# A decoder layer whose exponentials two engines share: a VectorE unit in every chunk, and the accumulators turned straight from their banks

## The chip, the cores and the metric

One core of one Trainium2 chip. The metric is the device time of one execution in microseconds (us). A time of the kernel is the median of its runs.

## The reference, cut to what matters

One decoder layer on x (1024 rows of 128) with a context of 6404 rows of 128. Three parts follow one another: a small self-attention with layer norm, a cross-attention with 16 heads of depth 8 over the context, and a quantised feed-forward part. The change is in the cross-attention, which takes most of the time:

```
qh = split_heads(q @ Wq + bq); kh = split_heads(k @ Wk + bk); vh = split_heads(v @ Wv + bv)
logits = einsum('bhsd,bhtd->bhst', qh, kh) / sqrt(8)      # 16 heads x 1024 x 6404
attn = softmax(logits, axis=-1)
out = einsum('bhst,bhtd->bhsd', attn, vh)                 # then @ Wo + bo
```

The kernel makes exp(logits) without a row maximum (a bound on the scores is computed first; a general path exists that these inputs don't take), multiplies it with the values and a column of ones, and divides by the sum that this column gives.

## The kernel before, in words

**Tiling.** The cross-attention is a stream of 8 phases: a phase is one half of the queries (512 columns) and a group of 4 heads (16 heads, so 4 groups; `PHASES` = 8). The context is 51 tiles of 128 rows (the last one short), 3 tiles to a chunk, so 17 chunks a phase (`NC`). A *unit* of scores is one tile for one head: 128 x 512 in one PSUM bank. Three units are a *block* (`BU`), 4 blocks a chunk (`BPC`), and the last chunk has 3 (`LAST_BPC`), since in its last tile the few rows of all four heads are packed into one unit. So a phase is 67 blocks (`BPP`), and the stream 536.

**Banks.** Blocks take turns in banks 0 to 2 and 3 to 5. Banks 6 and 7 (`ACC`) are the accumulators of the values.

**Who does what.** For every block TensorE multiplies the scores (`scores`, 12 matmuls, L1544) into its three banks; ScalarE takes the exponential of the three banks in one instruction (`exponentials`, L801, 128 x 1536) and writes it to `probs`, a ring of 8 blocks; TensorE multiplies `probs` with the values of the previous chunk (`values`, L1574). In `chunk`, TensorE's order for block s is written out by hand: wait, scores of block s, then a share of the values of the chunk before. The scores of a block wait for ScalarE to have finished the block two before it (`probs_ready`).

**VectorE's units.** In one block of a chunk, the third (`E_BLOCK` = 2), the last bank isn't ScalarE's: ScalarE's instruction there covers 128 x 1024 (`shared`, L805), and VectorE makes the exponential of that bank with a polynomial in 12 instructions, six steps of two halves of 256 columns. `take(ph, c)` (L1134) reads the bank in the first four (L1142 `e_t`, L1148 `e_f`); then the bank is free. `power(ph, c)` (L1152) does the rest (L1159, L1164, L1170, L1175) and writes into `probs`. GpSimd makes the power of two from `e_t` (`powers`, L667). Each of the first ten instructions raises `e_step` by one; each of the last two raises `e_probs`. Before, chunk 1 and the last chunk of a phase have no such unit: `e_count(ph, c)` counts 15 units a phase, 120 in all.

**What TensorE waits for.** At s = 0 of every chunk but the first of a phase it waits until the take of the chunk before is done (`E_TAKEN` = 4 steps), and before the values that read a unit's result it waits for `e_probs`:

```
if s == 0 and c:
    wait(e_step, at(E_STEPS * (e_count(ph, c - 1) - 1) + E_TAKEN, E_STEPS))
wait(probs_ready, at(f + s + 1, BPC))
...
scores(m % KS, q, ph, c == NC - 1, s)
```

In chunk 1 (before) this wait on chunk 0's take is the last of its phase's start, and at the start of chunk 2 `e_count(ph, 1)` gives the same unit of chunk 0 again.

**The end of a phase.** The values of the last chunk are multiplied in chunk 0 of the next phase, one tile each in its blocks 0, 1 and 2. Then VectorE adds the two accumulator banks into `acc_sb` (`add_acc`, L1125, between the take and the power of chunk 0), and after the power of chunk 0 turns them, divides and turns back (`turn_acc`, L1180, and L1198); SP stores the rows. TensorE begins the new phase's values at (c = 1, s = 1) and before them waits for the two steps of `add_acc` (`acc_step`, ACC_STEPS * (ph - 1) + 2). GpSimd stages the values of each chunk (`stage`, L660) and makes the powers, in the order of chunks.

## Time and profile before

| | us |
|---|---|
| median of 3 runs (782.94 to 783.8) | 783.37 |
| the profiled execution's own time | 783.59 |
| its span, first to last instruction | 781.9 |
| ScalarE busy | 730.6 |
| TensorE busy | 702.9 |
| VectorE busy | 601.3 |
| GpSimd busy | 179.7 |

The span is a little shorter than the time, as it leaves out what lies before the first and after the last instruction. Busy time of TensorE is modelled from matmuls that overlap, so a share of 90% doesn't say how far it is from its own limit. L801 is line 801 of the kernel before.

### The profile page before, as it was taken

The numbers are of one execution on the slowest core, as the hardware profiler recorded it, in microseconds if no ns is written. First come the engines' busy times: TensorE is split into PE (matmuls) and PEld (weight loads), VectorE is DVE, ScalarE is ACT, GpSimd is POOL, SyncE is SP. The second block draws the span as 40 slices with busy tenths as digits, with TensorE's granted clock in tenths as the row PEclk, the third lists the DMA queues.
The fourth block names the chain that finished last, engine by engine and source line by source line (L and its number), as shares of the span: only waits on it lengthen the run. The fifth ranks groups of instructions, "written<-read, shape, count | busy, mean of one in ns | idle before, by whom it ended". The sixth has DMA issues, their size and how long they took to land.

```text
span 781.9 us, 36725 instructions
## 1 busy us (share of the span) xinstructions
PE 702.9 (90%) x15175; PEld 315.3 (40%) x15179; DVE 601.3 (77%) x1719; ACT 730.6 (93%) x651; POOL 179.7 (23%) x322
## 2 busy tenths in 40 slices
PE   9998999999999999899998999999998999899985
PEld 4564344334443444344433443344433443344342
DVE  4668688858885888678867888588867886788877
ACT  3467999999999999999999999999999999999964
POOL 4437122212221222112211222122212222122201
PEclk9999999999999999999999999999999999999998
DMA  5364111111111111111111111111111111111000
GB/s 140 118 179 161 36 47 36 37 43 43 37 37 41 48 39 34 39 47 42 36 40 43 44 35 37 45 46 36 37 40 46 42 35 40 39 37 36 14 2 27
DMA packets 37044, 38.37 MB, mean 49 GB/s; under 512 B 8968, under 2 KB 35402, under 8 KB 36948
## 3 DMA queue, kind: packets, MB, share of 16 engines
q1 hardware_dynamic: 35840, 36.52, 15.7%
q8 instruction: 65, 1.06, 0.6%
q10 hardware_dynamic: 1108, 0.53, 0.2%
q14 instruction: 31, 0.25, 0.1%
HBM read 30.14 MB, written 6.42 MB: 47 GB/s over the span
## 4 chain that ended last, share of the span: by engine, by line
ACT 57%; issue 26%; PE 10%; DVE 3%; ACTq 1%; DMA 1%; DVEq 0%; POOL 0%; POOLq 0%
ACT probs L801 57%; PE ps L1438 2%; PE ps L1391 1%; PE ps L1399 1%; PE ps L1429 1%; PE ps L1574 1%; DMA wq_sb<-in_L_xattn_Wq_dram 1%; PE ps L1382 1%; ACTq L814 1%; PE ps L1544 1%; PE ps L1364 1%; DVE gmax L1241 0%; ACTq L799 0%; DVE probs L1301 0%; DVE stats L906 0%
## 5 line engine op out<-in xcount | busy, mean ns | idle before, releaser
L801 ACT ACTIVATE probs<-ps 128x1536 f32<-128x1536 f32 (+1 forms) x536 | 669.4, 1392 | 2.0 <-PE ps L1544 1.9
L1574 PE MATMUL ps<-probs,v_op 64*9 64x512 f32 (+1 forms) x8256 | 522.9, 496 | 0.0
L1544 PE MATMUL ps<-q_op,k_op 59*32 59x512 bf16 x6432 | 332.8, 379 | 62.0 <-ACT probs L801 59.6
L1544 PEld LDWEIGHTS ps<-q_op,k_op 59*32 59x32 bf16 x6432 | 102.2, 89 | 347.0 <-issue 257.0
L1142 DVE TENSOR_SCALAR e_t<-ps 128x256 f32<-128x256 f32 x240 | 90.7, 420 | 140.9 <-PE ps L1544 140.9
L1574 PEld LDWEIGHTS ps<-probs,v_op 64*9 64x9 f32 x8256 | 171.6, 86 | 61.4 <-issue 4.3
L667 POOL TENSOR_SCALAR e_pow<-e_t 128x512 int32<-128x512 int16 x120 | 74.6, 622 | 356.3 <-DVE e_t L1142 356.3
L660 POOL COPY v_op<-v_all 128x108 f32<-128x108 f32 x136 | 64.7, 476 | 167.5 <-PE ps L1574 167.0
L1170 DVE SCALAR_TENSOR_TENSOR e_f<-e_f,e_pow 128x256 f32<-128x256 f32 x240 | 98.5, 449 | 0.0
L1164 DVE SCALAR_TENSOR_TENSOR e_f<-e_u,e_f 128x256 f32<-128x256 f32 x240 | 90.2, 416 | 0.0
L1159 DVE SCALAR_TENSOR_TENSOR e_u<-e_f 128x256 f32<-128x256 f32 x240 | 90.0, 416 | 0.2
L1175 DVE SCALAR_TENSOR_TENSOR probs<-e_u,e_f 128x256 f32<-128x256 f32 x240 | 89.6, 411 | 0.0
L1148 DVE SCALAR_TENSOR_TENSOR e_f<-ps,e_t 128x256 f32<-128x256 f32 x240 | 89.3, 414 | 0.0
L737 ACT ACTIVATE probs<-ps,neg_n 128x1024 f32<-128x1024 f32 x8 | 8.9, 1114 | 18.9 <-PE ps L1429 18.9
L961 DVE SCALAR_TENSOR_TENSOR probs<-ps,bias_cols,k_parts 128x384 f32<-128x384 f32 x17 | 10.5, 615 | 17.7 <-ACT k_parts L723 10.3
L1364 PE MATMUL ps<-zeros_bf 128*128 128x512 bf16 x48 | 15.6, 455 | 1.5 <-DVE zeros_bf L932 1.3
L621 POOL TENSOR_TENSOR k_parts<-probs,k_parts 128x384 bf16<-128x384 f32 x17 | 15.5, 914 | 1.4
L1391 PE MATMUL ps<-ctx_t,wk_turned 128*128 128x384 f32 x34 | 14.8, 518 | 0.7 <-DVE probs L961 0.7
L619 POOL CAST k_parts<-probs 128x384 bf16<-128x384 f32 x17 | 8.6, 505 | 29.4 <-DVE probs L961 29.2
L1438 PE MATMUL ps<-probs,x_nat 128*128 128x512 f32 x32 | 15.1, 593 | 0.0
L1399 PEld LDWEIGHTS ps<-wv_sb,ctx_t 128*128 128x128 f32 x102 | 13.6, 191 | 3.4 <-issue 0.5
L1399 PE MATMUL ps<-wv_sb,ctx_t 128*128 128x128 f32 x102 | 14.0, 275 | 0.0
(201 smaller groups left out, 265.4 us busy)
## 6 DMA issues: line engine op xcount, KB each, us to landing
k_op<-k_parts_dram SPq DMA_DIRECT2D x544, 36.0 KB
k_parts_dram<-k_parts SPq DMA_DIRECT2D x17, 288.0 KB, 2.9
k_op<-k_parts_dram SPq DMA_DIRECT2D x272, 12.0 KB
ctx_nat<-in_ctx_dram SPq DMA_DIRECT2D x16, 192.0 KB, 3.3
q_op<-q_parts_dram SPq DMA_DIRECT2D x32, 48.0 KB
q_parts_dram<-q_parts SPq DMA_DIRECT2D x2, 384.0 KB, 3.5
x_nat<-in_x_dram SPq DMA_DIRECT2D x1, 512.0 KB, 3.9
o_t<-att_rows SPq DMA_DIRECT2D x28, 16.0 KB
```

The costliest lines, as they stand in the source:

```text
L660: pool.tensor_copy(v_op[:, slot].rearrange("p j (h d) -> p j h d", h=G), v_all[:, bass.ds(tile, CT), head:head + G, :]).then_inc(v_staged, 1)
L667: pool.tensor_scalar(e_pow[:], e_low(e_t[:]), float(2 ** 23), float(EXP2_LEAD), ALU.mult, ALU.add).then_inc(e_pow_ready, 1)
L801: act.activation(probs[:, b % NP].rearrange("p u t -> p (u t)")[:, 0:columns], ps[:, bank:bank + BU, :].rearrange("p u t -> p (u t)")[:, 0 ...
L1142: dve.tensor_scalar(e_t[:, cols], score, E_MIN, ROUND + EXP2_OFF, ALU.max, ALU.add).then_inc(e_step, 1)
L1148: dve.scalar_tensor_tensor(out=e_f[:, cols], in0=score, scalar=E_MIN, in1=e_low(e_t[:, cols]), op0=ALU.max, op1=ALU.subtract).then_inc(e_s ...
L1159: dve.scalar_tensor_tensor(out=e_u[:, cols], in0=e_f[:, cols], scalar=a, in1=e_f[:, cols], op0=ALU.add, op1=ALU.mult).then_inc(e_step, 1)
L1164: dve.scalar_tensor_tensor(out=e_f[:, cols], in0=e_u[:, cols], scalar=d, in1=e_f[:, cols], op0=ALU.add, op1=ALU.mult).then_inc(e_step, 1)
L1170: dve.scalar_tensor_tensor(out=e_f[:, cols], in0=e_f[:, cols], scalar=e, in1=e_pow[:, cols].bitcast(F32), op0=ALU.add, op1=ALU.mult).then_ ...
L1175: dve.scalar_tensor_tensor(out=probs[:, block % NP, BU - 1, 512 - EW + cols.start:512 - EW + cols.stop], in0=e_u[:, cols], scalar=b, in1=e ...
L1399: last = pe.matmul(ps[:, v_bank(n), P * j:P * j + P], ctx_t[:, n % 3, P * j:P * j + P], wv_sb[:], start=True, stop=True)
L1544: return pe.matmul(ps[a:a + P // G, bank, :], k_op[W2 * r:W2 * r + KR, kslot, i, P * j + a:P * j + a + P // G], q_op[W2 * r:W2 * r + KR, q ...
L1574: last = pe.matmul(ps[32 * k:32 * k + DH + 1, ACC[h], a:b], v_op[W2 * h:W2 * h + W2, slot, j, (DH + 1) * k:(DH + 1) * (k + 1)], probs[W2 * ...
```

## The change

It does four things.

- `E_UNITS` goes from 15 to 17: VectorE makes a unit in every chunk. Only the last chunk of the last phase has none (`e_made`). In chunk 1 the unit is the last bank of the fourth block (`e_block(1)` = 3), in the others it stays in the third. ScalarE's instructions there shrink to 128 x 1024, and GpSimd makes a power of two for each new unit.
- TensorE gets a wait at (c = 0, s = 1) for the take of the last chunk of the phase before. Its wait at s = 0 of every other chunk stays as it is.
- The values of the packed tile (the last tile of the last chunk) are multiplied in block 3 of chunk 0 and no longer in block 2, behind a wait for the last chunk's unit.
- The accumulators are no longer copied and added, then turned: VectorE turns each from its bank (`turn_acc`, two transposes of 128 x 512, between the first and the second factor of chunk 0's unit), adds the kept columns and takes the reciprocal after chunk 2's unit (`divide_acc`), multiplies after chunk 3's (`normalise_acc`), and turns back after chunk 4's (`turn_rows`). `power` is split into `first_factor`, `second_factor` and `power`, with the same instructions. `ACC_STEPS` stays 5, and TensorE's wait for two steps now covers the two transposes.

```diff
--- before.py
+++ after.py
@@ -78,7 +78,7 @@
 EW = 512
 EH = EW // 2
 E_BLOCK = BPC - 2
-E_UNITS = NC - 2
+E_UNITS = NC
 EXP2_OFF = 2
 EXP2_LEAD = 0x3a8bec00 - EXP2_OFF * 2 ** 23
 EXP2 = [9.525652885437012, 28.199888229370117, 45.54460906982422, 132.23011779785156]
@@ -302,7 +302,15 @@
 
         def e_count(ph, c):
 
-            return ph * E_UNITS + max(c - 1, 0) + 1
+            return ph * E_UNITS + c + 1
+
+        def e_block(c):
+
+            return BPC - 1 if c == 1 else E_BLOCK
+
+        def e_made(ph, c):
+
+            return c < NC - 1 or ph < PHASES - 1
 
         def e_low(ap):
 
@@ -671,7 +679,7 @@
                 for c in range(NC):
                     m = ph * NC + c
                     stage(m % 2, m, c * CT, ph % NG * G)
-                    if c != 1 and c < NC - 1:
+                    if e_made(ph, c):
                         powers(ph, c)
 
 
@@ -802,20 +810,21 @@
                                ps[:, bank:bank + BU, :].rearrange("p u t -> p (u t)")[:, 0:columns],
                                ACT.Exp, scale=1.0 / LOG2E).then_inc(probs_ready, 1)
 
-            def shared(s):
-                return BU * 512 - EW if s == E_BLOCK else BU * 512
+            def shared(s, c=0):
+                return BU * 512 - EW if s == e_block(c) else BU * 512
 
             for ph in range(PHASES):
                 f = ph * BPP
                 for s in range(BPC):
                     exponentials(f + s, f + (s + 1 + AHEAD), shared(s))
                 for s in range(BPC, 2 * BPC):
-                    exponentials(f + s, f + (s + 1 + AHEAD))
-                with act.Fori(0, E_UNITS // 2) as r:
+                    exponentials(f + s, f + (s + 1 + AHEAD), shared(s - BPC, 1))
+                with act.Fori(0, (NC - 3) // 2) as r:
                     for s in range(2 * BPC, 4 * BPC):
                         exponentials(f + s, r * (2 * BPC) + (f + s + 1 + AHEAD), shared(s % BPC))
                 for s in range((NC - 1) * BPC, BPP):
-                    exponentials(f + s, f + (s + 1 + AHEAD))
+                    exponentials(f + s, f + (s + 1 + AHEAD),
+                                 shared(s % BPC) if e_made(ph, NC - 1) else BU * 512)
 
 
             act.preload_act_table(ACT.Sqrt)
@@ -1122,18 +1131,18 @@
             with dve.If(dve.value_load(flag[0:1, 0:1]) > 0):
                 general_shift_dve(dve)
 
-            def add_acc(ph):
+            def turn_acc(ph):
 
                 dve.wait_ge(values_done, V_AHEAD + VPC * NC * (ph + 1))
-                acc_chain.step(dve.tensor_copy(acc_sb[:], ps[:, ACC[0], :]))
-                acc_chain.step(dve.tensor_tensor(acc_sb[:], acc_sb[:], ps[:, ACC[1], :], ALU.add))
+                acc_chain.step(dve.transpose(acc_t[:].rearrange("p n d -> p (n d)"), ps[:, ACC[0], :]))
+                acc_chain.step(dve.transpose(acc_sb[:], ps[:, ACC[1], :]))
 
             acc_chain = Chain(dve, acc_step)
             halves = (slice(0, EH), slice(EH, EW))
 
             def take(ph, c):
 
-                block = ph * BPP + c * BPC + E_BLOCK
+                block = ph * BPP + c * BPC + e_block(c)
                 bank = BU * (block % 2) + BU - 1
                 done = E_STEPS * (e_count(ph, c) - 1)
                 dve.wait_ge(scores_done, block + 1 + AHEAD)
@@ -1149,21 +1158,29 @@
                                              in1=e_low(e_t[:, cols]), op0=ALU.max, op1=ALU.subtract
                                              ).then_inc(e_step, 1)
 
-            def power(ph, c):
-
-                block = ph * BPP + c * BPC + E_BLOCK
+            def first_factor(ph, c):
+
                 done = E_STEPS * (e_count(ph, c) - 1)
-                a, b, d, e = EXP2
                 for n, cols in enumerate(halves):
                     dve.wait_ge(e_step, done + 2 + n + 1)
-                    dve.scalar_tensor_tensor(out=e_u[:, cols], in0=e_f[:, cols], scalar=a,
+                    dve.scalar_tensor_tensor(out=e_u[:, cols], in0=e_f[:, cols], scalar=EXP2[0],
                                              in1=e_f[:, cols], op0=ALU.add, op1=ALU.mult
                                              ).then_inc(e_step, 1)
+
+            def second_factor(ph, c):
+
+                done = E_STEPS * (e_count(ph, c) - 1)
                 for n, cols in enumerate(halves):
                     dve.wait_ge(e_step, done + 4 + n + 1)
-                    dve.scalar_tensor_tensor(out=e_f[:, cols], in0=e_u[:, cols], scalar=d,
+                    dve.scalar_tensor_tensor(out=e_f[:, cols], in0=e_u[:, cols], scalar=EXP2[2],
                                              in1=e_f[:, cols], op0=ALU.add, op1=ALU.mult
                                              ).then_inc(e_step, 1)
+
+            def power(ph, c):
+
+                block = ph * BPP + c * BPC + e_block(c)
+                done = E_STEPS * (e_count(ph, c) - 1)
+                b, e = EXP2[1], EXP2[3]
                 for n, cols in enumerate(halves):
                     dve.wait_ge(e_step, done + 6 + n + 1)
                     dve.wait_ge(e_pow_ready, e_count(ph, c))
@@ -1177,28 +1194,39 @@
                         in0=e_u[:, cols], scalar=b, in1=e_f[:, cols], op0=ALU.add, op1=ALU.mult
                         ).then_inc(e_probs, 1)
 
-            def turn_acc():
-                acc_chain.step(dve.transpose(acc_t[:].rearrange("p n d -> p (n d)"), acc_sb[:]))
+            def divide_acc():
+                both = [acc_t[:, :, 0:DH + 1], acc_sb[:].rearrange("p (n d) -> p n d", d=R)[:, :, 0:DH + 1]]
+                acc_chain.step(dve.tensor_tensor(both[0], both[0], both[1], ALU.add))
                 acc_chain.step(dve.reciprocal(att_rden[:], acc_t[:, :, DH]))
+
+            def normalise_acc():
                 acc_chain.step(dve.tensor_tensor(
                     acc_t[:, :, 0:DH], acc_t[:, :, 0:DH],
                     bass.AP(att_rden[:].tensor, att_rden[:].offset,
                             [list(att_rden[:].ap[0]), [1, HQ // R], [0, DH]]), ALU.mult))
 
+            def turn_rows(ph):
+                if ph > 1:
+
+                    dve.wait_ge(o_written, 16 * G * (ph - 1))
+                dve.transpose(att_rows[:], acc_t[:].rearrange("p n d -> p (n d)")).then_inc(att_ready, 1)
+
             for ph in range(PHASES):
-                take(ph, 0)
-                if ph:
-                    add_acc(ph - 1)
-                power(ph, 0)
-                if ph:
-                    turn_acc()
-                    if ph > 1:
-
-                        dve.wait_ge(o_written, 16 * G * (ph - 1))
-                    dve.transpose(att_rows[:], acc_t[:].rearrange("p n d -> p (n d)")).then_inc(att_ready, 1)
-                for c in range(2, NC - 1):
+                for c in range(NC):
+                    if not e_made(ph, c):
+                        continue
                     take(ph, c)
+                    first_factor(ph, c)
+                    if ph and c == 0:
+                        turn_acc(ph - 1)
+                    second_factor(ph, c)
                     power(ph, c)
+                    if ph and c == 2:
+                        divide_acc()
+                    if ph and c == 3:
+                        normalise_acc()
+                    if ph and c == 4:
+                        turn_rows(ph)
 
 
             dve.wait_ge(x1_bo_ready, 1)
@@ -1593,6 +1621,9 @@
                     pe.wait_ge(signal, count)
 
                 for s in range(LAST_BPC if c == NC - 1 else BPC):
+                    if s == 1 and c == 0 and ph:
+
+                        pe.wait_ge(e_step, E_STEPS * (e_count(ph - 1, NC - 1) - 1) + E_TAKEN)
                     if s == 0 and c:
 
                         wait(e_step, at(E_STEPS * (e_count(ph, c - 1) - 1) + E_TAKEN,
@@ -1616,8 +1647,10 @@
 
                         wait(v_staged, at(m, 1))
                     if c == 0:
-                        if s < CT:
-                            values(slot, f - LAST_BPC, s, True, count=2 if s == 1 else 1)
+                        if s == BPC - 1:
+                            pe.wait_ge(e_probs, 2 * e_count(ph - 1, NC - 1))
+                        if s != 2:
+                            values(slot, f - LAST_BPC, min(s, 2), True, count=2 if s == 1 else 1)
                     elif c == NC - 1:
                         if s == 2:
                             pe.wait_ge(e_probs, 2 * e_count(ph, c - 1))
```

## Rows read from the trace of the kernel before

**Rows 1.** The page: span; busy us (share), instructions by engine

```profile
span 781.9 us, 36725 instructions
...
PE 702.9 (90%) x15175; PEld 315.3 (40%) x15179; DVE 601.3 (77%) x1719; ACT 730.6 (93%) x651; POOL 179.7 (23%) x322
```

**Rows 2.** The page: the chain that ended last, by engine

```profile
ACT 57%; issue 26%; PE 10%; DVE 3%; ACTq 1%; DMA 1%; DVEq 0%; POOL 0%; POOLq 0%
```

**Rows 3.** Windows, chunks 0, 1, 3, 16: length, busy by engine, clock, DMA

```profile
241.99:246.97 4.98, 4.20 (x84) 1.04 (x72) 2.65 (x6) 4.98 (x5) 0.90 (x2) 1.00 0.15 41
246.97:252.30 5.33, 4.99 (x112) 1.70 (x112) 4.70 (x13) 5.33 (x6) 0.28 (x1) 1.00 0.15 42
257.38:262.33 4.95, 4.47 (x126) 2.12 (x112) 4.17 (x14) 4.95 (x6) 1.14 (x3) 1.00 0.17 48
321.60:325.59 3.99, 3.99 (x100) 1.55 (x84) 1.48 (x5) 3.99 (x4) 0.48 (x2) 1.00 0.14 43
```

**Rows 4.** Groups by line and form, ScalarE: busy us, mean ns, idle

```profile
L801 ACT ACTIVATE probs<-ps 128x1536 f32<-128x1536 f32 x416 | 574.3, 1485 | 2.0 <-PE ps L1544 1.9
L801 ACT ACTIVATE probs<-ps 128x1024 f32<-128x1024 f32 x120 | 128.4, 1070 | 0.0
```

**Rows 5.** The chain, phases 1 to 2: start us, us, what

```profile
238.00 12.61 ACT probs L801 x10
...
250.97 1.08 ACT probs L801
...
252.30 1.09 ACT probs L801
```

**Rows 6.** Timeline, VectorE, one unit and the next: start us, us

```profile
230.36 0.75 DVE L1142 TENSOR_SCALAR e_t<-ps 128x256 f32<-128x256 f32 x2 [0.69 <-PE ps L1544]
...
233.03 0.82 DVE L1170 SCALAR_TENSOR_TENSOR e_f<-e_f,e_pow 128x256 f32<-128x256 f32 x2
233.78 0.75 DVE L1175 SCALAR_TENSOR_TENSOR probs<-e_u,e_f 128x256 f32<-128x256 f32 x2
235.31 0.76 DVE L1142 TENSOR_SCALAR e_t<-ps 128x256 f32<-128x256 f32 x2 [0.78 <-PE ps L1544]
```

**Rows 7.** Timeline, all engines, chunk 16 into chunk 0

```profile
239.91 0.37 PE L1544 MATMUL ps<-q_op,k_op 59*32 59x512 bf16 x1
...
241.02 0.61 PE L1544 MATMUL ps<-q_op,k_op 59*32 59x512 bf16 x12
...
243.62 0.61 PE L1544 MATMUL ps<-q_op,k_op 59*32 59x512 bf16 x12
...
244.28 0.76 DVE L1142 TENSOR_SCALAR e_t<-ps 128x256 f32<-128x256 f32 x2 [4.81 <-PE ps L1544]
...
244.96 0.74 DVE L1148 SCALAR_TENSOR_TENSOR e_f<-ps,e_t 128x256 f32<-128x256 f32 x2
...
245.12 0.62 POOL L667 TENSOR_SCALAR e_pow<-e_t 128x512 int32<-128x512 int16 x1 [3.53 <-DVE e_t L1142]
```

**Rows 8.** Groups by line and form, VectorE, 100 to 740 us

```profile
L1181 DVE STREAM_TRANSPOSE acc_t<-acc_sb 128x512 f32<-128x512 f32 x7 | 4.9, 701 | 0.0
...
L1128 DVE COPY acc_sb<-ps 128x512 f32<-128x512 f32 x7 | 4.7, 678 | 0.0
L1183 DVE TENSOR_TENSOR acc_t<-acc_t,att_rden 128x128 f32<-128x128 f32 x7 | 2.0, 292 | 0.2
L1182 DVE RECIPROCAL att_rden<-acc_t 128x16 f32<-128x16 f32 x7 | 1.8, 254 | 0.2
```

**Rows 9.** Timeline, TensorE, scores with a full tile between

```profile
206.40 0.61 PE L1544 MATMUL ps<-q_op,k_op 59*32 59x512 bf16 x12 [0.30 <-ACT probs L801]
...
207.55 0.52 PE L1544 MATMUL ps<-q_op,k_op 59*32 59x512 bf16 x5
```

**Rows 10.** Timeline, TensorE, the scores of block 3 of chunk 1

```profile
249.91 0.61 PE L1544 MATMUL ps<-q_op,k_op 59*32 59x512 bf16 x12
```

**Rows 11.** Waits, 90 to 740 us: us in total, times, longest

```profile
PEld ps L1544 <- DVE e_f L1148: 15.7, 31, 0.9
```

## The prediction

> **What bounds the kernel now.** I read the page's busy line first: ScalarE (ACT) is busy for 93% of a span of 781.9 us, TensorE (PE) for 90%, VectorE (DVE) for 77% [rows 1]. Shares over a whole span do not say which of three busy engines sets the pace, so I went to the chain that ended last: 57% of it is ScalarE's exponential L801, 26% is issue, and VectorE has 3% [rows 2]. Then the windows, one chunk of stream each. In every window ScalarE is busy for the whole length (4.98 of 4.98, 5.33 of 5.33, 3.99 of 3.99) while PE has 4.2 to 5.0 and VectorE 1.5 to 4.7; the granted clock is 1.00, the 2.4 GHz level [rows 3]. So the stream runs at ScalarE's pace: eight phases of 83.6 us. What counts is when ScalarE starts each block, and anything that makes it wait is paid in full.
>
> I write (c,s) for block s of chunk c, and use the clock of phase 2, whose (0,0) starts at 241.99. A full block takes ScalarE 1.33 us from start to start (250.97 to 252.30); the ten from 238.00 to 250.97, one of them cut, are 9 x 1.33 + 0.98 [rows 5]. The records themselves are longer (1485 ns full, 1070 ns cut [rows 4]) as they overlap, so I go by starts.
>
> **The gain.** Two chunks of a phase have no VectorE unit before: chunk 1 takes 5.33 us where chunk 3 with a unit takes 4.95, a gain of 0.38 for one unit [rows 3]. The change adds 15 units: eight in chunk 1, seven in the last chunk (phases 0 to 6). By this alone the sum would be 15 x 0.38 = 5.7 us. The records' difference, 1485 - 1070 = 415 ns, would give 6.2 us [rows 4]; the chunk falls short of it because the block behind a cut one waits for its scores.
>
> The Trainium skill ("Vector Engine (DVE) Microarchitecture Reference", the passage on rate slope and fixed cost) gives the scalar engine 0.833 ns per column: 512 columns fewer would be 0.427 us, 6.4 us in all, an estimate from that page. The records agree (0.415); the chunk windows (0.38) differ, and the measurement decides.
>
> **The price of a unit on VectorE.** Six pairs of halves take from 230.36 to 234.53 (233.78 + 0.75), 4.17 us; the next unit starts at 235.31, so 0.78 us of a chunk is idle [rows 6]. Taking the scores out of their bank is the first four instructions: 244.28 to 245.70 (244.96 + 0.74), 1.42 us [rows 7]. VectorE starts 0.05 us after the last score (243.62 + 0.61 = 244.23, then 244.28), and GpSimd 0.08 us after VectorE's pair (245.04 to 245.12) [rows 7]. No row has PE held by a take alone; I take 0.12 from its end to the first score: GpSimd's 0.08 and 0.04 for a weight load. Bounds are 0.05, the quickest handover, and 0.20.
>
> **Chunk 16 into chunk 0 (phases 1 to 7).** The scores of (16,2) end at 240.28 (239.91 + 0.37) [rows 7], ScalarE starts that block at 238.00 + 2 x 1.33 = 240.66 [rows 5], and the scores of (0,0) end at 241.63 [rows 7]. With the block cut, ScalarE can start (0,0) 0.05 behind those scores, at 241.68 in place of 241.99: a gain of 0.31, not 0.38. VectorE works on unit 16 from 240.32 to 244.50. The scores of (0,2), moved 0.31 earlier, end at 243.92, so take 0 begins late, at 244.53, and ends at 245.95. PE's wait at (1,0) then lets its scores run 246.07 to 246.68, and ScalarE starts (1,0) at 246.73. Undelayed it would start at 246.66 (244.34 + 0.98 + 1.34, the cut block of this chunk being 4.98 - 3 x 1.33 = 0.98 [rows 3], the block behind it 1.34). Stall: 0.07.
>
> The new wait at (0,1) costs nothing: take 16 ends at 241.74, and PE has values to multiply until about then. The packed tile's values go from (0,2) to (0,3), behind unit 16's end (244.50) and the scores of (0,3) (about 245.3), so their new wait costs nothing either; if unit 16 were over 0.7 us later, it would.
>
> **The accumulators.** A copy, an add of all 512 columns and a transpose become two transposes and an add of the kept 144 columns. A transpose out of PSUM is in no row. The copy out of PSUM takes 678 ns and the transpose out of SBUF 701 [rows 8], so I take 0.71 each with its step, 0.70 to 0.80. They begin behind take 0 and the first factor, at 244.53 + 2.01 = 246.54, and end at 247.97. PE waits for them at (1,1), before its values. With ScalarE's (1,0) at 246.73, the scores of (1,1) end at about 247.7, so the values start at 248.05, 0.35 late. PE's own pace with a full tile of values is 1.15 us a block (206.40 to 207.55), 0.61 of it scores [rows 9]. So scores of (1,2) start at 248.05 + 0.54 = 248.59 and end at 249.20, in time for ScalarE (249.39), but scores of (1,3) start at 249.74 and end at 250.35. Before they ended at 250.52 (249.91 + 0.61) [rows 10]: only 0.17 of the 0.31 is left there. Divide, normalise and rows go behind units 2, 3 and 4: at 0.29 (the nearest is the product of 128 columns) + 0.25, 0.29 and 0.70 us [rows 8] against 0.78 idle in each [rows 6]. They cost nothing; the last leaves 0.08, and even a lag of 0.3 would be hidden at PE's gate. SP's stores of the rows come two chunks later and have most of a phase.
>
> **Chunk 1 into chunk 2, the step that decides.** The unit of chunk 1 is in block (1,3), but PE still waits for its take before the scores of (2,0), as after every chunk. Elsewhere the unit is in (c,2) and a whole block lies between. Here nothing does. In bank terms (1,3) is freed for (2,1), so this wait is a block stricter than the data ask. Take 1 runs 250.39 to 251.81; scores of (2,0) 251.93 to 252.54; ScalarE starts (2,0) at 252.59. Before it started at 252.30 [rows 5]. So a phase is **0.29 us longer**, in spite of two cut blocks: 0.31 + 0.38 gained, 0.98 lost, most of it in this one place. The cut only lets ScalarE arrive sooner at the wait. In phase 0 the scores of (1,3) come where they came, 250.52 on this clock: take 250.57 to 251.99, scores 252.11 to 252.72, start 252.77, that is +0.47. Unit 1 ends at 254.56, before the scores of (2,2), and from chunk 3 on the pace is the old one.
>
> **Sum:** 7 x 0.29 + 0.47 = 2.5 us. The profiled execution took 783.59 (span 781.9 [rows 1] and 1.7 around it), 0.22 over the median of 783.37. So 783.37 + 2.5 = **785.9**. Bounds: with handovers of 0.05 and no accumulator delay a phase is +0.1 and phase 0 +0.4, 784.5; with transposes of 0.80, handovers of 0.20 and PE at 1.25 a block, +0.55 and +0.55, 787.8.
>
> **Rivals.** About 0.2% (1.6 us) is what a measurement of this kernel can tell from no change.
>
> 1. *The gate at (2,0) is covered: faster.* It decides if all stalls of a phase together stay under 0.69 us, what two cuts gain. Then PE must be able to start (2,0)'s scores by 251.6, 1.3 us after (1,3)'s. If the gate cost nothing, 5.7 us less the loss on chunk 16 (7 x 0.07) and the small stalls (7 x 0.07) would be left: 778.7; at the records' 0.415 us a unit and without any loss, 777.2 [rows 4]. For it: in the waits of before, VectorE's take is named 31 times for 15.7 us of weight load [rows 11], in 118 chunks with a unit, and ScalarE has no gap for it. Against it: a take is 1.42 us of dependent work that cannot start before (1,3)'s scores end. Chance 0.10. This is also what the skill's rate of 0.833 ns per column would give if ScalarE alone set the time, 783.4 - 6.4 = 777.0, again an estimate from that page.
>
> 2. *About even.* As forecast, but the accumulators are ready in time and the handovers quick: per phase +0.1 to +0.15, 784.4 to 784.9. Chance 0.25.
>
> 3. *VectorE falls behind: slower by more.* It was busy for 4.17 us of a chunk's 4.95 [rows 3] and now is for nearly all of chunks 2 to 4, and GpSimd's copies now run beside units. If instructions stretch by 10% there, the lag of 0.6 at chunk 0 grows through chunks 1 to 4 and each take delays PE by some 0.2: 8 x 4 x 0.1 = 3 us more, 789. For: one pair of each unit, the one with GpSimd's powers, already takes 0.82 against 0.75 [rows 6]. Against: units with that overlap already take the 4.17 us I used. Chance 0.10.
>
> 4. *The cut at (16,2) gives nothing,* as PE is already busy for 3.99 of 3.99 us there [rows 3]. Then a phase loses the 0.31 too, but the take of chunk 0 is less late: about 787.5. Chance 0.07, within the forecast's upper end.
>
> **The numbers.** The forecast in its own range (784.5 to 787.8) has 0.48, and the rivals the rest. The range to hold the time 8 times in 10 must take in even results, a gate that is half covered (0.4 us less in 8 phases, 3.2 us: 782.7) and part of the worse ones: 782.7 to 788.4. Faster by over 0.2%: 0.10. Within 0.2%: 0.26 (rival 2 and the lower end of the forecast). Slower: 0.64.
>
> **What would show it.** In the profile after: 135 cut blocks and 401 full ones at L801; ScalarE idle before (2,0) in every phase, some 0.6 to 1.0 us, with PE's scores named, and PE there waiting for VectorE's second subtraction; chunk 1 of about 5.7 to 5.9 us where it was 5.33, chunk 16 of about 3.7; chunk 3 onward 4.95 as before; VectorE busy for some 660 us. The forecast is wrong if ScalarE does not wait before (2,0), if chunks 3 to 15 grow, or if chunk 0 grows by more than 0.2.

## The result and the profile after

| | median us | runs |
|---|---|---|
| before | 783.49 | 6, 782.74 to 783.88 |
| changed | 787.67 | 6, 787.53 to 788.34 |

The ratio is 1.0053, with a 95% interval of 1.0042 to 1.0064: the change makes the kernel slower by 4.2 us or 0.5%, little, but clear of the noise.

The page of the changed kernel: span, busy us by engine, and the chain that ended last.

```profile
span 785.8 us, 36972 instructions
...
PE 697.8 (89%) x15175; PEld 318.1 (40%) x15179; DVE 659.8 (84%) x1899; ACT 725.7 (92%) x651; POOL 187.6 (24%) x337
...
ACT 44%; issue 26%; PE 17%; DVE 12%; ACTq 1%; DVEq 0%
```

Against [rows 1, 2], ScalarE is busy for 4.9 us less, as it should be with 15 smaller instructions, and the span is 3.9 us longer. ScalarE's share of the chain fell from 57% to 44%, VectorE's rose from 3% to 12%. So ScalarE now waits.

Windows of phase 2, chunks 0, 1, 2 and 16, cut at ScalarE's starts (length, then busy of PE, PEld, DVE, ACT, POOL, and the clock):

```profile
242.69:247.64 4.95, 4.19 (x88) 1.24 (x72) 4.95 (x16) 4.95 (x6) 1.46 (x4) 1.00 0.16 43
247.64:253.99 6.35, 4.71 (x104) 1.97 (x112) 5.72 (x16) 5.16 (x5) 0.98 (x2) 1.00 0.15 40
253.99:258.94 4.95, 4.60 (x124) 2.29 (x112) 4.43 (x15) 4.95 (x5) 0.94 (x2) 1.00 0.16 43
323.16:326.84 3.68, 3.68 (x92) 1.55 (x84) 2.84 (x10) 3.68 (x4) 0.72 (x2) 1.00 0.16 47
```

Chunk 1 is the only one that grew: 6.35 us where it was 5.33 [rows 3], and ScalarE is busy for 5.16 of it. Chunk 16 fell from 3.99 to 3.68. VectorE is busy for every bit of chunk 0.

Groups by line and form:

```profile
L809 ACT ACTIVATE probs<-ps 128x1536 f32<-128x1536 f32 x401 | 556.0, 1466 | 11.3 <-PE ps L1572 11.1
...
L809 ACT ACTIVATE probs<-ps 128x1024 f32<-128x1024 f32 x135 | 142.4, 1055 | 0.0
...
L1138 DVE STREAM_TRANSPOSE acc_sb<-ps 128x512 f32<-128x512 f32 x7 | 5.0, 717 | 0.2
...
L1137 DVE STREAM_TRANSPOSE acc_t<-ps 128x512 f32<-128x512 f32 x7 | 4.9, 701 | 0.0
```

The counts are as forecast, 401 full blocks and 135 cut ones; [rows 4] had 416 and 120. ScalarE's idle before full blocks went from 2.0 to 11.3 us. The transposes out of PSUM take 701 and 717 ns, so they cost what the one out of SBUF costs [rows 8].

The timeline from chunk 0's take to chunk 2 (phase 2 starts at 242.69 here, so 1.01 is to be taken off to compare with the times of the prediction as it moved the phase's start to 241.68; the bracket is idle time and what ended it):

```profile
245.42 0.74 DVE L1151 TENSOR_SCALAR e_t<-ps 128x256 f32<-128x256 f32 x2
...
246.09 0.73 DVE L1157 SCALAR_TENSOR_TENSOR e_f<-ps,e_t 128x256 f32<-128x256 f32 x2
...
246.88 0.61 PE L1572 MATMUL ps<-q_op,k_op 59*32 59x512 bf16 x12
...
247.42 0.70 DVE L1137 STREAM_TRANSPOSE acc_t<-ps 128x512 f32<-128x512 f32 x1
...
248.15 0.72 DVE L1138 STREAM_TRANSPOSE acc_sb<-ps 128x512 f32<-128x512 f32 x1
...
248.92 1.07 PE L1602 MATMUL ps<-probs,v_op 64*9 64x512 f32 x16 [0.42 <-DVE acc_sb L1138]
...
249.79 0.59 PE L1572 MATMUL ps<-q_op,k_op 59*32 59x512 bf16 x9
...
250.87 0.64 PE L1572 MATMUL ps<-q_op,k_op 59*32 59x512 bf16 x12
...
251.57 0.76 DVE L1151 TENSOR_SCALAR e_t<-ps 128x256 f32<-128x256 f32 x2 [0.57 <-PE ps L1572]
252.24 0.74 DVE L1157 SCALAR_TENSOR_TENSOR e_f<-ps,e_t 128x256 f32<-128x256 f32 x2
...
253.34 0.61 PE L1572 MATMUL ps<-q_op,k_op 59*32 59x512 bf16 x12 [0.97 <-DVE e_u L1166]
...
253.99 1.46 ACT L809 ACTIVATE probs<-ps 128x1536 f32<-128x1536 f32 x1 [1.17 <-PE ps L1572]
```

The reader is to see two places. At 248.92 TensorE's values of (1,1) have waited for the transposes; its next scores, those of (1,2), start at 249.79. And (1,3)'s scores end at 251.51 (250.87 + 0.64), VectorE takes them from 251.57 to 252.98, TensorE starts (2,0)'s scores only at 253.34 and ScalarE starts that block at 253.99, after 1.17 us of idling. The waits over the stream, which name them:

```profile
ACT probs L809 <- PE ps L1572: 8.2, 7, 1.2
PE ps L1572 <- DVE e_u L1166: 6.8, 7, 1.0
...
PE ps L1602 <- DVE acc_sb L1138: 2.9, 7, 0.4
```

7 waits of ScalarE, 1.2 us the longest, 8.2 us in all: the 7 full phases that the window holds. TensorE's wait there is put down to `e_u` L1166, as that was the last VectorE instruction to come before it; what the code waits for is the take ahead of it.

### The profile page after: what moved, and what is told of

It is laid out like the page before. It is cut to its first block, busy times and chain, and to the rows that moved or that the text cites. A ratio compares the mean times of both kernels' runs of the same rounds, so it can differ in the third digit from the quotient of the medians.

```text
span 785.8 us, 36972 instructions
## 1 busy us (share of the span) xinstructions
PE 697.8 (89%) x15175; PEld 318.1 (40%) x15179; DVE 659.8 (84%) x1899; ACT 725.7 (92%) x651; POOL 187.6 (24%) x337
## 4 chain that ended last, share of the span: by engine, by line
ACT 44%; issue 26%; PE 17%; DVE 12%; ACTq 1%; DVEq 0%
ACT probs L809 42%; PE ps L1602 5%; PE ps L1572 3%; DVE e_t L1151 2%; DVE e_f L1157 2%; PE ps L1466 2%; DVE e_u L1166 2%; PE ps L1419 1%; PE ps L1427 1%; PE ps L1457 1%; PE ps L1410 1%; DVE e_f L1187 1%; DVE acc_sb L1138 1%; PE ps L1392 1%; DVE probs L1192 1%
## 5 line engine op out<-in xcount | busy, mean ns | idle before, releaser
L809 ACT ACTIVATE probs<-ps 128x1536 f32<-128x1536 f32 (+1 forms) x536 | 664.5, 1362 | 11.3 <-PE ps L1572 11.1
L1572 PEld LDWEIGHTS ps<-q_op,k_op 59*32 59x32 bf16 x6432 | 107.3, 90 | 341.1 <-issue 261.5
L1602 PEld LDWEIGHTS ps<-probs,v_op 64*9 64x9 f32 x8256 | 168.1, 86 | 68.2 <-DVE acc_sb L1138 6.3
L675 POOL TENSOR_SCALAR e_pow<-e_t 128x512 int32<-128x512 int16 x135 | 83.9, 622 | 415.7 <-DVE e_t L1151 415.7
L1151 DVE TENSOR_SCALAR e_t<-ps 128x256 f32<-128x256 f32 x270 | 101.9, 419 | 87.3 <-PE ps L1572 86.8
L1187 DVE SCALAR_TENSOR_TENSOR e_f<-e_f,e_pow 128x256 f32<-128x256 f32 x270 | 108.8, 441 | 0.0
L1175 DVE SCALAR_TENSOR_TENSOR e_f<-e_u,e_f 128x256 f32<-128x256 f32 x270 | 102.6, 420 | 0.2
L1166 DVE SCALAR_TENSOR_TENSOR e_u<-e_f 128x256 f32<-128x256 f32 x270 | 102.2, 419 | 0.0
L1192 DVE SCALAR_TENSOR_TENSOR probs<-e_u,e_f 128x256 f32<-128x256 f32 x270 | 100.8, 411 | 0.0
L1157 DVE SCALAR_TENSOR_TENSOR e_f<-ps,e_t 128x256 f32<-128x256 f32 x270 | 100.4, 413 | 0.0
```

The source lines that it names most:

```text
L675: pool.tensor_scalar(e_pow[:], e_low(e_t[:]), float(2 ** 23), float(EXP2_LEAD), ALU.mult, ALU.add).then_inc(e_pow_ready, 1)
L809: act.activation(probs[:, b % NP].rearrange("p u t -> p (u t)")[:, 0:columns], ps[:, bank:bank + BU, :].rearrange("p u t -> p (u t)")[:, 0 ...
L1151: dve.tensor_scalar(e_t[:, cols], score, E_MIN, ROUND + EXP2_OFF, ALU.max, ALU.add).then_inc(e_step, 1)
L1157: dve.scalar_tensor_tensor(out=e_f[:, cols], in0=score, scalar=E_MIN, in1=e_low(e_t[:, cols]), op0=ALU.max, op1=ALU.subtract).then_inc(e_s ...
L1166: dve.scalar_tensor_tensor(out=e_u[:, cols], in0=e_f[:, cols], scalar=EXP2[0], in1=e_f[:, cols], op0=ALU.add, op1=ALU.mult).then_inc(e_ste ...
L1175: dve.scalar_tensor_tensor(out=e_f[:, cols], in0=e_u[:, cols], scalar=EXP2[2], in1=e_f[:, cols], op0=ALU.add, op1=ALU.mult).then_inc(e_ste ...
```

## The experiments

All times are medians; "against before" is the ratio to the kernel before on the same chip with its 95% interval. The last columns are lengths in phase 2, from ScalarE's starts. The experiments ran in several groups, each beside runs of the kernel before of its own; these had medians of 783.19 to 783.40, and 783.49 beside the changed kernel. In the traces what lies ahead of the stream of exponentials varies by 0.8 us from kernel to kernel, and what lies behind it by 0.4. So a difference of two medians is good to some tenths of a us, and a smaller one is read from the lengths of the phases. In the diffs of this section the lines that matter stand alone: counts, loops and ScalarE's widths that follow from them are cut.

| kernel | us | against before | chunk 1 | chunk 2 | chunk 16 | phase |
|---|---|---|---|---|---|---|
| before | 783.49 | | 5.32 | 5.08 | 3.99 | 83.60 |
| changed | 787.67 | 1.0053 (1.0042 to 1.0064) | 6.36 | 4.95 | 3.69 | 84.16 |
| gate_moved | 781.02 | 0.9972 (0.9962 to 0.9981) | 5.20 | 5.25 | 3.66 | 83.30 |
| chunk2_peeled | 785.72 | 1.0034 (1.0021 to 1.0048) | 6.08 | 4.91 | 3.65 | 83.88 |
| no_unit_chunk1 | 781.30 | 0.9970 (0.9957 to 0.9982) | 5.50 | 4.95 | 3.69 | 83.31 |
| no_unit_last | 789.53 | 1.0095 (1.0074 to 1.0115) | 6.11 | 4.94 | 3.99 | 84.34 |
| no_new_units | 783.45 | 1.0002 (0.9992 to 1.0011) | 5.32 | 5.00 | 3.99 | 83.60 |
| unit1_block2 | 782.30 | 0.9985 (0.9976 to 0.9994) | 5.73 | 4.94 | 3.69 | 83.53 |
| acc_first | 786.46 | 1.0043 (1.0028 to 1.0058) | 6.13 | 4.94 | 3.69 | 83.93 |
| acc_copied | 804.79 | 1.0279 (1.0263 to 1.0294) | 8.02 | 5.69 | 3.69 | 86.56 |
| gate_acc | 780.13 | 0.9961 (0.9946 to 0.9976) | 5.39 | 4.92 | 3.64 | 83.19 |
| block3_acc | 780.72 | 0.9965 (0.9953 to 0.9977) | 5.39 | 4.94 | 3.72 | 83.23 |
| block2_peeled_acc | 783.01 | 0.9999 (0.9990 to 1.0008) | 5.83 | 4.91 | 3.66 | 83.63 |
| gate_split | 779.56 | 0.9944 (0.9929 to 0.9959) | 5.05 | 5.15 | 3.65 | 83.04 |

**The gate before (2,0): gate_moved.** Its edit to the changed kernel, with chunk 2 taken out of TensorE's loop (next experiment):

```diff
+                    if s == 1 and c == 2:
+                        pe.wait_ge(e_step, E_STEPS * (e_count(ph, 1) - 1) + E_TAKEN)
-                    if s == 0 and c:
+                    if s == 0 and c and c != 2:
```

> The changed kernel with one edit that matters: TensorE waits for chunk 1's take before the scores of (2,1) and not before those of (2,0); for that chunk 2 is taken out of TensorE's loop. Theory A (the strict wait before (2,0) is what turns the gain into a loss): in the changed kernel ScalarE starts (2,0) 2.19 us after (1,3), where a cut block needs about 0.95; so some 1.2 us a phase, 9.5 us in 8 phases, comes back, less 0.2 to 0.3 us a phase, as unit 2 now finds VectorE still at unit 1 and its take delays (3,0): 779.5 to 781. Theory B (VectorE is too full, any wait it is freed from returns at the next take): 785 or more, with the waits now before (3,0) and (4,0).

781.02: 6.65 us less than the changed kernel, and below the kernel before. That settles theory A against B in the main: the wait for chunk 1's take, a block stricter than the banks ask, is what turned the gain into a loss. It lies 0.02 above the upper end of what A gave: 0.34 us came back at the next take, where 0.2 to 0.3 were expected, and (2,0) starts 1.03 us behind (1,3), not 0.95. gate_moved's timeline at chunk 2's take:

```profile
253.26 0.75 DVE L1192 SCALAR_TENSOR_TENSOR probs<-e_u,e_f 128x256 f32<-128x256 f32 x2
253.94 0.74 DVE L1151 TENSOR_SCALAR e_t<-ps 128x256 f32<-128x256 f32 x2
...
254.60 0.74 DVE L1157 SCALAR_TENSOR_TENSOR e_f<-ps,e_t 128x256 f32<-128x256 f32 x2
...
255.69 0.61 PE L1572 MATMUL ps<-q_op,k_op 59*32 59x512 bf16 x12 [0.27 <-DVE e_u L1166]
...
256.35 1.46 ACT L809 ACTIVATE probs<-ps 128x1536 f32<-128x1536 f32 x1 [0.20 <-PE ps L1572]
```

Unit 2 starts at 253.94, while unit 1's last instruction is ending (253.26 + 0.75), with no idle time between: VectorE is late. The take ends at 255.34, TensorE starts (3,0) at 255.69, ScalarE at 256.35, 1.67 us behind the block before, where 1.33 is due. To that extent theory B has a point: VectorE has no room left there.

**The loop's part: chunk2_peeled.**

```diff
                 chunk(ph, 1)
+                chunk(ph, 2)
                 with pe.Fori(0, (NC - 5) // KS) as i:
-                    for c in range(2, 2 + KS):
+                    for c in range(3, 3 + KS):
                         chunk(ph, c, i, KS)
-                for c in range(NC - 3, NC):
+                for c in range(NC - 2, NC):
```

> The changed kernel with chunk 2 taken out of TensorE's loop (the loop runs over chunks 3 to 14), every wait where it was. The control for gate_moved. Theory C: from the end of the take at (1,3) to the first score of (2,0) pass 0.36 us, where the same wait at (1,0), outside of a loop, passes in 0.06; that is the loop's waits on register values, so outside of the loop (2,0) starts 0.2 to 0.3 us earlier in each phase: 785.3 to 786.1. If the 0.36 has another cause (VectorE, memory), the time stays at 787.7.

785.72, as expected by theory C. In its timeline:

```profile
251.33 0.75 DVE L1157 SCALAR_TENSOR_TENSOR e_f<-ps,e_t 128x256 f32<-128x256 f32 x2
...
252.13 0.61 PE L1572 MATMUL ps<-q_op,k_op 59*32 59x512 bf16 x12 [0.68 <-DVE e_f L1157]
...
252.80 1.45 ACT L809 ACTIVATE probs<-ps 128x1536 f32<-128x1536 f32 x1 [0.88 <-PE ps L1572]
```

The take ends at 252.08 (251.33 + 0.75) and the scores start 0.05 us later, where the changed kernel had 0.36 in the loop. In gate_moved the wait before (3,0), in the loop again, has 0.35. So 0.28 us a phase of the changed kernel's loss (84.16 to 83.88) is the place of this wait, the first of a loop whose counts are worked out in registers. It isn't only the first wait of the loop that is dear. In the kernel before, blocks 2 and 3 of a chunk wait for ScalarE alone, and by the records TensorE starts their scores 0.14 us after the end of the exponential waited for in chunks 2 to 13, which are inside the loop (all 192 cases), and 0.05 us after it in chunks 14 and 15, which are behind it (all 32). Block 0 has two such waits, for the take and for ScalarE. Of gate_moved's 6.65 us, 1.95 are the peeling and 4.70 the moved gate.

**Each unit alone: no_unit_chunk1 and no_unit_last.**

```diff
-            return c < NC - 1 or ph < PHASES - 1
+            return c != 1 and (c < NC - 1 or ph < PHASES - 1)
```

> The changed kernel without the unit of chunk 1 (ScalarE makes that whole block; 127 units in all), the last chunk's unit and the accumulators as changed. Theory A: the wait before (2,0) asks for chunk 0's take, long done; chunk 1 goes back to 5.33 us and the accumulators' wait at (1,1); the last chunk still gains 0.30 in 7 phases: against before -0.30 and about +0.15 for the late accumulators, 7 times, 782.0 to 783.2. If the loss lies in the last chunk's unit or in the accumulators, 785 to 787.

```diff
-            return c < NC - 1 or ph < PHASES - 1
+            return c < NC - 1
-                    if s == 1 and c == 0 and ph:
-                        pe.wait_ge(e_step, E_STEPS * (e_count(ph - 1, NC - 1) - 1) + E_TAKEN)
-                        if s == BPC - 1:
-                            pe.wait_ge(e_probs, 2 * e_count(ph - 1, NC - 1))
```

> The changed kernel without the last chunk's unit (128 units), chunk 1's in the fourth block with the strict gate. Theory A: the gate takes the same 1.2 us a phase, the 0.30 us of the last chunk's cut is gone 7 times, and unit 0 starts on time, which gives back some 0.1 us before (1,0) and 0.16 before (1,2): 787.7 to 788.7. If the last chunk's unit had cost more than it gains, 787 or less.

Without chunk 1's unit the kernel is at 781.30, 6.4 us faster than with it, and better than expected, as chunk 2 takes 4.95 where before had 5.08. Without the last chunk's unit it is at 789.53, 1.9 us slower, and 0.8 slower than expected: the 0.30 us of each cut in chunk 16 is real and worth 2.1 us, and of the 0.26 us that unit 0's punctual start was to give back, chunk 1 shows 0.25 less (6.11 for 6.36) but chunk 0 0.12 more (5.07 for 4.95). So of the two new units one pays and one costs, and the one that costs is chunk 1's behind its strict gate.

**The rest of the change alone: no_new_units** (both edits above).

> The changed kernel without any of the new units (120, as before): what is left is the accumulators turned from their banks and the packed tile's values a block later. By my sum these cost nothing by themselves: unit 0 starts on time, the transposes end before TensorE wants them; 783.2 to 784.0. In no_unit_last chunk 0 took 5.07 us where before had 4.98; if that stays, 7 x 0.09 = 0.6 us more than before, 784.0.

783.45, ratio 1.0002: without new units the turned accumulators and the packed tile's later values cost and gain nothing that can be measured. Chunk 0 does take 5.07 us where before had 4.98, as feared, but chunk 2 takes 5.00 where before had 5.08.

**Chunk 1's unit in the third block: unit1_block2.**

```diff
-            return BPC - 1 if c == 1 else E_BLOCK
+            return E_BLOCK
```

> The changed kernel with chunk 1's unit in the third block as in all others, the gate before (2,0) untouched. Between the units of chunks 0 and 1 there are now 4 blocks (4.95 us) for 4.17 + 1.42 us of VectorE's work, on top of the lag of about 0.4 with which unit 0 starts. Unit 1 then starts some 1.1 to 1.3 us late and its take ends 2.6 to 2.8 us after the scores of (1,2), where ScalarE wants (2,0)'s scores to start by 2.0: a stall of 0.6 to 0.9 us in phases 1 to 7 and none in phase 0, and a smaller one before (3,0). Theory A: that is less than the 1.24 us of the strict gate: 784 to 786.5. Theory B (fullness of VectorE is the limit): 787.5 or more.

782.30, 0.15% faster than before and 5.4 us faster than the changed kernel, and so below the range that even theory A gave (784 to 786.5). Its timeline:

```profile
249.61 0.74 DVE L1151 TENSOR_SCALAR e_t<-ps 128x256 f32<-128x256 f32 x2
...
250.28 0.74 DVE L1157 SCALAR_TENSOR_TENSOR e_f<-ps,e_t 128x256 f32<-128x256 f32 x2
...
251.40 0.61 PE L1572 MATMUL ps<-q_op,k_op 59*32 59x512 bf16 x12 [0.34 <-DVE e_u L1166]
...
252.06 1.45 ACT L809 ACTIVATE probs<-ps 128x1536 f32<-128x1536 f32 x1 [0.34 <-PE ps L1572]
```

I had the take 1.1 to 1.3 us behind its scores. It is 0.5 behind (they end at 249.11), as the late accumulators hold (1,2)'s scores back too (they start at 248.48, behind values that waited for the transposes until 247.61). ScalarE idles 0.34 us before (2,0), where the changed kernel has 1.17. Moving the unit one block on, away from VectorE's crowd, put it against the gate.

**The accumulators: acc_first, acc_copied.** acc_first has the transposes directly behind the take; acc_copied has in addition copy and add for the two transposes, and the old transpose, reciprocal, product and transpose behind unit 0.

```diff
                     take(ph, c)
-                    first_factor(ph, c)
                     if ph and c == 0:
                         turn_acc(ph - 1)
+                    first_factor(ph, c)
```

> The changed kernel with the two transposes of the accumulators directly behind chunk 0's take, ahead of the first factor (as the copy and add stood before the change). They end 0.67 us earlier, so TensorE's values at (1,1) are not held (1.0 us from 247.9 to 248.9 in the changed kernel), ScalarE doesn't wait before (1,2) (0.16 us) and the scores of (1,3) come about 0.4 us earlier. Since (2,0) starts at a fixed distance behind those scores, each of 7 phases is 0.3 to 0.45 us shorter: 784.5 to 785.6. If the accumulators' wait is hidden by the gate at (2,0), 787.6.

> The changed kernel with the accumulators handled as before: copy and add directly behind chunk 0's take, and transpose, reciprocal, product and transpose behind its last factor. This puts 2.0 us of work between unit 0 (which ends 0.5 us before unit 1 can start in the changed kernel) and unit 1, so its take ends some 1.2 to 1.5 us later and TensorE's gate before (2,0) with it: 7 x 1.2 to 1.5, 795 to 798. If VectorE had room there, 787.7 or less.

acc_first: 786.46, 0.23 us a phase, less than the 0.3 to 0.45 I gave it, and outside the range (784.5 to 785.6); the wait before (1,2) is gone, but VectorE came to the transposes before TensorE was done with the packed tile's values and idled for 0.33 us. Its waits have it 7 times:

```profile
DVE acc_t L1137 <- PE ps L1602: 2.3, 7, 0.3
```

acc_copied: 804.79, worse than the worst I gave (798). VectorE around unit 1, and ScalarE's waits:

```profile
253.49 0.75 DVE L1192 SCALAR_TENSOR_TENSOR probs<-e_u,e_f 128x256 f32<-128x256 f32 x2
...
255.51 0.71 DVE L1211 STREAM_TRANSPOSE att_rows<-acc_t 128x512 f32<-128x512 f32 x1
256.14 0.72 DVE L1151 TENSOR_SCALAR e_t<-ps 128x256 f32<-128x256 f32 x2
256.79 0.74 DVE L1157 SCALAR_TENSOR_TENSOR e_f<-ps,e_t 128x256 f32<-128x256 f32 x2
```

```profile
ACT probs L809 <- PE ps L1569: 24.5, 12, 3.4
```

Unit 1's take begins when the last transpose is done and ends at 257.53; the scores of (1,3) were done at 254.07. The stalls then reach into chunk 2 (5.69 us). So the shift of this work behind chunks 2 to 4 is, in the main, what makes the unit in chunk 1 bearable at all: acc_copied takes 17 us more than the changed kernel and 18 more than acc_first, while without the new units the old and the new handling take the same time (no_new_units against before).

**Together: gate_acc, block3_acc, block2_peeled_acc.** gate_acc has gate_moved's and acc_first's edits. block3_acc puts the units of chunks 1 to 14 in the fourth block:

```diff
-            return BPC - 1 if c == 1 else E_BLOCK
+            return BPC - 1 if 0 < c < NC - 2 else E_BLOCK
-                    if s == 0 and c:
+                    if s == (1 if 1 < c < NC - 1 else 0) and c:
```

> gate_moved and acc_first together. With the gate moved, ScalarE still waits 0.16 us before (1,2) for the late accumulators, and 0.74 us before (3,0), where unit 2's take is late because VectorE starts it only when unit 1 ends. Theory A1 (the lag at unit 2 comes from 3 blocks between the units of chunks 1 and 2, 3.6 us, for 4.17 us of work): the accumulators' place doesn't change it, only the 0.16 us goes: 7 x 0.16 = 1.1 us, 779.9. Theory B1 (the lag is carried over from chunk 0's accumulators): more than 2 us.

> gate_acc, and the units of chunks 1 to 14 all in the fourth block with their gates at s = 1, so that no two units are 3 blocks apart there; the step back to the third block is between chunks 14 and 15, outside of TensorE's loop. Theory A1: ScalarE's wait of 0.74 us before (3,0) goes, and a smaller one, 0 to 0.3 us, comes before (16,0): 8 x 0.45 to 0.75 less than gate_acc, 774 to 777. If the lag is VectorE's own fullness, it shows before (16,0) at the same size and the time is gate_acc's.

gate_acc's 780.13 is close to what A1 gave (779.9), but by luck: A1 had the delay before (3,0) stay. Its timeline:

```profile
244.08 0.74 DVE L1157 SCALAR_TENSOR_TENSOR e_f<-ps,e_t 128x256 f32<-128x256 f32 x2
...
245.15 0.72 DVE L1137 STREAM_TRANSPOSE acc_t<-ps 128x512 f32<-128x512 f32 x1 [0.33 <-PE ps L1602]
...
248.67 0.76 DVE L1192 SCALAR_TENSOR_TENSOR probs<-e_u,e_f 128x256 f32<-128x256 f32 x2
249.34 0.75 DVE L1151 TENSOR_SCALAR e_t<-ps 128x256 f32<-128x256 f32 x2
...
249.48 1.07 PE L1602 MATMUL ps<-probs,v_op 64*9 64x512 f32 x16 [0.22 <-DVE probs L1192]
...
251.02 1.45 ACT L809 ACTIVATE probs<-ps 128x1536 f32<-128x1536 f32 x1 [0.33 <-PE ps L1572]
```

The wait before (3,0) is gone (chunk 2 takes 4.92 us, in gate_moved 5.25), as the accumulators now come earlier, and a new one of 0.33 us stands before (2,0) (chunk 1 takes 5.39, in gate_moved 5.20): VectorE idles before the transposes (245.15), unit 0 ends late, at 249.43, and TensorE's values of (1,3) wait for it. So the lag at unit 2 did hang on the place of the accumulators, as B1 had it, and only the sum of the two shifts, 0.11 us a phase, looks like A1. The 0.74 us that both expectations put before (3,0) isn't in gate_moved's trace either: ScalarE starts (3,0) there 1.67 us behind a full block, where 1.33 is due, so 0.34 is lost, 0.20 of it idle. So block3_acc, expected at 774 to 777, had nothing left to win before (3,0); it came out level with gate_acc (780.72; the intervals overlap). Its premise, and the size taken for it, were wrong. block2_peeled_acc is unit1_block2 with the peeled chunk and acc_first:

> unit1_block2 (chunk 1's unit in the third block, gates at s = 0) with chunk 2 out of TensorE's loop and the accumulators' transposes directly behind the take. If the parts add as they did in the changed kernel (chunk2_peeled took 0.28 us off a phase, acc_first 0.23 off 7): 782.3 - 2.2 - 1.6 = 778.5. If VectorE's order is the limit (unit 0 ends where it did, so unit 1's take begins no earlier), acc_first gives nothing here: 779.6 to 780.3. Theory B (what is freed returns): 782.

783.01, a plain miss: slower than unit1_block2, although both edits helped in the changed kernel. Unit 1's take starts 8.65 us into the phase (249.31 - 240.66) where unit1_block2 had 8.23 (249.61 - 241.38). The 0.33 us idle before the transposes is passed on to unit 1, and with gates at s = 0 unit 1 is what ScalarE waits for. TensorE's start behind the take came down from 0.38 to 0.06 us by the peeling, as it should, but a take 0.42 us later costs more than that: chunk 1 is 5.83 us, in unit1_block2 5.73.

**The gap filled: gate_split.**

```diff
                 for n, cols in enumerate(halves):
+                    if n and between:
+                        between()
...
-                    first_factor(ph, c)
-                    if ph and c == 0:
-                        turn_acc(ph - 1)
+                    first_factor(ph, c, (lambda: turn_acc(ph - 1)) if ph and c == 0 else None)
```

> gate_moved with the accumulators' transposes between the two halves of chunk 0's first factor. Directly behind the take (gate_acc, block2_peeled_acc) VectorE sits idle 0.33 us until TensorE has multiplied the packed tile's values, and then unit 0 ends late, TensorE waits for it before the values of (1,3) and ScalarE for TensorE before (2,0) (1.39 us behind (1,3), where about 1.0 is a cut block). Half a factor (0.33 us) fills just that gap. If that is right: VectorE's idle gap before the transposes is gone, unit 0 ends 0.3 us earlier, (2,0) starts about 0.3 us earlier and unit 1 and 2 too: 0.2 to 0.35 us in 7 phases less than gate_acc's 780.1: 777.7 to 778.7. If another wait comes up in its place, 780.

779.56, the fastest of all, 0.9944 of before. VectorE's part is as expected, the gain is not: 0.15 us a phase against gate_acc (83.19 to 83.04) and not 0.2 to 0.35, and the time lies outside the 777.7 to 778.7 expected, near the 780 given for another wait coming up in its place. The intervals of the two ratios overlap, so that gate_split is faster rests on the phases. VectorE in chunks 0 and 1, and windows of chunks 0 to 2:

```profile
244.06 0.74 DVE L1157 SCALAR_TENSOR_TENSOR e_f<-ps,e_t 128x256 f32<-128x256 f32 x2
244.72 0.41 DVE L1168 SCALAR_TENSOR_TENSOR e_u<-e_f 128x256 f32<-128x256 f32 x1
245.13 0.72 DVE L1137 STREAM_TRANSPOSE acc_t<-ps 128x512 f32<-128x512 f32 x1
...
248.32 0.75 DVE L1194 SCALAR_TENSOR_TENSOR probs<-e_u,e_f 128x256 f32<-128x256 f32 x2
249.30 0.76 DVE L1151 TENSOR_SCALAR e_t<-ps 128x256 f32<-128x256 f32 x2 [0.23 <-PE ps L1572]
```

```profile
240.67:245.62 4.95, 4.18 (x88) 1.24 (x72) 4.95 (x15) 4.95 (x6) 1.34 (x4) 1.00 0.14 40
245.62:250.66 5.04, 4.62 (x105) 1.80 (x112) 4.74 (x14) 5.04 (x5) 0.52 (x1) 1.00 0.16 42
250.66:255.81 5.15, 4.66 (x120) 1.84 (x112) 5.15 (x17) 5.06 (x6) 1.47 (x4) 1.00 0.16 43
```

The gap before the transpose is gone, unit 0 ends at 249.07 where gate_acc had 249.43 with the phase at the same place (240.67 and 240.68), and from unit 16 to the gate before (3,0) VectorE idles once, for 0.23 us. It is busy for all of chunks 0 and 2. The other wait is the one before (3,0) again, 0.16 us of TensorE for the take of unit 2 and 0.09 of ScalarE (255.81), with chunk 2 at 5.15 us where gate_acc had 4.92. There VectorE has no time left to give: this stretch now has two bounds.

## Why the prediction was right, and where its sizes were off

The prediction had slower, 785.9, in a range of 782.7 to 788.4; measured were 787.67, and 4.2 us more where 2.5 were forecast. The mechanism was right, two of its terms were too small, and a gain that it didn't have hid part of that.

- **What bounds the kernel, and the gain of a cut.** Right. Chunk 16 gained 0.30 of the 0.31 us forecast, and from chunk 3 on all is as before. That TensorE has 4.2 to 5.0 us in every window leaves out chunk 16, where it is busy for all of the 3.99 us [rows 3]; the cut block gained its time there all the same.
- **Chunk 16 into chunk 0.** Right: take 0 began 2.73 us into the phase (245.42 - 242.69) where 2.85 were forecast, and (1,0) started after 4.95 where 5.05 were. It costs nothing to speak of, and gave 0.03 us more in chunk 0.
- **The accumulators.** The transposes are 0.70 and 0.72 us, their end 6.18 us into the phase (forecast 6.29). But behind the hold TensorE took 0.87 us from the values to the next scores (248.92 to 249.79), not 0.54. The failed step is the reading of [rows 9]: I took the 0.61 us of the scores' record off the pace of 1.15 us and called the rest the values. In the kernel before the values between those two blocks of scores stand so:

```profile
206.69 1.18 PE L1574 MATMUL ps<-probs,v_op 64*9 64x512 f32 x16
```

They start 0.29 us after the scores (206.40), while these still run, and the next scores follow 0.86 us behind them (207.55). So a tile's values take as long in a fed queue as behind the hold. ScalarE lost 0.16 us before (1,2), and (1,3)'s scores ended at 8.82, not 8.67.
- **The gate before (2,0).** Right in place, cause and sign: gate_moved shows it. Chunk 1 came to 6.35 us, where 5.7 to 5.9 were given as the sign, and ScalarE's idle time to 1.17 us, where 0.6 to 1.0 were. The take lasts 1.41 us, as [rows 7] had it. The failed term is the handover: 0.12 us forecast, 0.20 its upper bound, 0.36 measured. The row I took it from has GpSimd waiting on a constant count; TensorE's wait here is the first of a loop with counts in registers, and chunk2_peeled shows 0.05 outside of it. The trace before had the price of one such wait, 0.14 us inside the loop against 0.05 outside; it had not been looked up.
- **The sum.** In a phase +0.29 was forecast and +0.56 measured: +0.24 by the handover, +0.15 by the accumulators, -0.13 since chunk 2 has 4.95 us and no longer 5.08, and 0.01 of rounding. What chunk 2 gained was not forecast, and it lies in its one cut block: from the start of (2,2) to that of (2,3) 1.07 us pass before and 0.92 after. The cause stays open. Without it the time would have been some 0.9 us more, 788.6, past the upper end of the range, so that the range held was in part luck. With 0.56 for 0.29 the old sum 7 x 0.29 + 0.47 = 2.5 becomes 7 x 0.56 + 0.5 = 4.4, and the stream (first to last exponential) is 4.4 us longer; the tail behind it is 0.3 us and the head 0.1 us shorter.
- **Rival 1** (covered gate) fell. It named the right point: with the wait moved the kernel is faster than before. But it gave 778.7, and even gate_split keeps 0.86 us over. The rate of 0.833 ns per column from the Trainium skill's "Vector Engine (DVE) Microarchitecture Reference" (section "Measured stream behaviour on trn2", rate slope and fixed cost) is 427 ns for 512 columns, and this trace agrees to 4%: 1466 - 1055 = 411 ns. By that rule alone the estimate was 777.0; no run came there. The rate prices ScalarE's instruction, and the time went to ScalarE's waiting.
- **Rival 2** (even) fell: neither were the accumulators in time nor the handover quick.
- **Rival 3** (VectorE falls behind in chunks 1 to 4) did not happen in the changed kernel, whose strict gate gives VectorE time to catch up. It is what remains once the gate is gone (gate_moved, gate_split).
- **Rival 4** fell: the cut at (16,2) gives its 0.30.

## What to carry to other kernels

When a piece of work is moved to a later slot, move the wait that frees its buffer with it: a wait one slot too strict can cost much of that work's latency (here 0.97 us of TensorE's idle time for a take of 1.41), and the time saved elsewhere only brings the fast engine sooner to the same wait. Price a wait by the code around it: in this kernel one in the loop, with a count from registers, cost more than one in straight code. And when two edits each helped, try them together before adding them up: an idle gap that one of them opens is paid by whatever is then on the path (block2_peeled_acc). And take the length of a step from start to start: the records of TensorE's matmuls overlap, so one can't be subtracted from the other.

## What I had not expected of the hardware

- TensorE starts scores 0.05 to 0.06 us behind the VectorE instruction it waits for in straight code (252.08 to 252.13 in chunk2_peeled; 246.82 to 246.88 in the changed kernel), and 0.35 to 0.38 us behind it at the entry of its loop (252.98 to 253.34 in the changed kernel; 255.34 to 255.69 in gate_moved; 251.02 to 251.40 in unit1_block2). Behind ScalarE, in blocks 2 and 3, it is 0.05 outside the loop and 0.14 inside. A wait in the loop has its count from register arithmetic, and this kernel puts a second wait, for a count long reached, ahead of it. What of this takes the time, or whether fetching does, wasn't separated.
- Two transposes of 128 x 512 out of PSUM take 0.70 and 0.72 us, as much as out of SBUF (0.70 and 0.71 in the kernel before).
- In four of the six kernels with chunk 2 peeled (gate_moved, gate_acc, gate_split, block2_peeled_acc) one chunk, always chunk 6 of phase 5, takes 5.26 or 5.27 us in place of 4.95. chunk2_peeled has no such chunk, block3_acc has one elsewhere (chunk 4 of phase 6, 5.25 us). The cause is open; it is 0.3 us in all.
